# Second attention stage of a fused decoder kernel: probabilities turned by VectorE blocks and DMAs, head outputs two tiles behind the scores

## The reference, cut to what matters

```python
    x = x + _L0_xattn_ref(_layernorm(x, axis=-1), ctx_1024, mask_BxS2_bk0, L0_xattn_W_Q, L0_xattn_W_K, L0_xattn_W_V, L0_xattn_W_O)
...
        Q = _split_heads(X_Q @ W_Q, KEY_SIZE)
        K = _split_heads(X_KV @ W_K, KEY_SIZE)
        V = _split_heads(X_KV @ W_V, VALUE_SIZE)
        E = jnp.einsum('bhqd,bhkd->bhqk', Q, K)
        E = jnp.where(key_padding_mask[:, None, None, :], -jnp.inf, E)
        A = jax.nn.softmax(E / jnp.sqrt(jnp.float32(KEY_SIZE)), axis=-1)
        Yp = jnp.einsum('bhqk,bhkd->bhqd', A, V)
...
        Y = Yp.transpose(0, 2, 1, 3).reshape(b, sq, h * dv) @ W_O
```

## Time and profile before

| | us |
|---|---|
| runs | 3205.45, 3195.68, 3205.67 |
| median | 3205.45 |
| profiled execution, its time | 3192.96 |
| its span, first to last instruction | 3190.9 |
| TensorE busy in it | 3112.9 |
| VectorE, ScalarE, GpSimd busy | 2767.5, 2517.5, 2330.3 |
| mean granted TensorE clock, share of full | 0.993 |
| first queries matmul of the second stage | at 176.15 |
| first TensorE instruction of the third stage | at 553.67 |

### The profile page before, as it was taken

The page is one execution under the profiler, slowest core; times in us unless marked ns, Lnnn a source line. Parts: engine busy times, 40 slices in busy tenths (PEclk is TensorE's granted clock), DMA queues, the critical chain, the costliest instruction groups (busy, mean ns, idle before and its releaser), DMA issues.

```text
span 3190.9 us, 125347 instructions
## 1 busy us (share of the span) xinstructions
PE 3112.9 (98%) x51271; PEld 2450.5 (77%) x51271; DVE 2767.5 (87%) x5489; ACT 2517.5 (79%) x5156; POOL 2330.3 (73%) x3927
## 2 busy tenths in 40 slices
PE   7999999899999999999999999999999999999997
PEld 5677787577777777777777777777777777777776
DVE  6844444899999999999999999999999999999996
ACT  6856665588888888888888888888888888888886
POOL 6732222788888888888888888888888888888885
PEclk9999999999999999999999999999999999999998
DMA  4000000565555655555655566555565555555552
GB/s 111 3 7 8 8 8 5 119 129 108 108 109 121 123 121 110 111 109 122 125 108 108 109 124 126 115 111 110 114 126 122 109 107 109 109 108 117 114 117 60
DMA packets 280547, 310.51 MB, mean 97 GB/s; under 512 B 154281, under 2 KB 225582, under 8 KB 279982
## 3 DMA queue, kind: packets, MB, share of 16 engines
q0 software_dynamic: 58368, 201.36, 34.1%
q1 hardware_dynamic: 220892, 100.93, 12.7%
q10 hardware_dynamic: 722, 0.21, 0.0%
HBM read 23.63 MB, written 2.10 MB: 8 GB/s over the span
## 4 chain that ended last, share of the span: by engine, by line
PE 86%; DVE 4%; ACT 3%; issue 2%; POOL 2%; SPq 1%; DMA 1%; POOLq 0%; ACTq 0%; DVEq 0%
PE bank L1173 10%; PE bank L1195 10%; PE bank L1141 10%; PE bank L1255 10%; PE bank L1229 8%; PE bank L1112 8%; PE bank L1244 6%; PE bank L1214 5%; PE bank L1128 4%; PE bank L1152 3%; PE bank L728 2%; PE bank L741 2%; PE bank L750 2%; PE bank L805 2%; PE bank L1209 1%
## 5 line engine op out<-in xcount | busy, mean ns | idle before, releaser
L1435 DVE TENSOR_TENSOR RK<-bank,tables 128x1024 f32<-128x1024 f32 x384 | 468.5, 1224 | 83.0 <-ACT sq L1320 75.4
L1421 DVE TENSOR_TENSOR RQ<-bank,q_tables 128x1024 f32<-128x1024 f32 x384 | 451.3, 1217 | 25.8 <-ACT sq L1314 11.9
L1569 POOL TENSOR_TENSOR RK<-RK,rn 128x512 f32<-128x512 f32 x384 | 400.9, 1045 | 86.5 <-DMA RK<-RK 72.8
L1575 POOL TENSOR_TENSOR P<-P,rn 128x512 f32<-128x512 f32 x384 | 395.2, 1050 | 6.0 <-DVE P L1485 5.9
L1173 PE MATMUL bank<-WA,xcT 128*128 128x512 f32 x768 | 394.9, 596 | 2.5 <-DVE P L1485 2.4
L1287 ACT ACTIVATE V<-bank 128x512 f32<-128x512 f32 x384 | 230.5, 600 | 209.0 <-PE bank L1244 208.4
L1581 POOL TENSOR_TENSOR P<-P,inv_sum 128x512 f32<-128x512 f32 x384 | 393.5, 1045 | 0.0
L1195 PE MATMUL bank<-WV,xcT 128*128 128x512 f32 x768 | 391.6, 605 | 0.0
L1555 POOL DMA_DIRECT2D RQ<-RQ x384 | 387.4, 1313 | 2.3 <-issue 2.3
L1141 PE MATMUL bank<-xcT,WQ 128*128 128x128 f32 x3072 | 375.9, 276 | 4.8 <-ACT xcT L1287 4.8
L1561 POOL DMA_DIRECT2D RK<-RK x192 | 175.4, 913 | 280.7 <-DVE RK L1435 267.2
(11 more groups left out here) (169 smaller groups left out, 7341.0 us busy)
## 6 DMA issues: line engine op xcount, KB each, us to landing
RK<-RK POOLq DMA_DIRECT2D x192, 512.0 KB, 5.4
RQ<-RQ POOLq DMA_DIRECT2D x384, 256.0 KB, 6.6
Z<-Z SPq DMA_DIRECT2D x768, 64.0 KB, 4.1
WA<-in_wqkv SPq DMA_DIRECT2D x24, 256.0 KB, 2.9
ystat<-Y SPq DMA_DIRECT2D x192, 32.0 KB
ystat<-Y SPq DMA_DIRECT2D x384, 15.8 KB
ys<-Y SPq DMA_DIRECT2D x192, 32.0 KB
ys<-Y SPq DMA_DIRECT2D x384, 15.8 KB
```

The costliest lines, as they stand in the source:

```text
L1421: tt(both, src.unsqueeze(1).to_broadcast([128, 2, 8, SEQ]), m.q_tables[:, layer(t), :, :].unsqueeze(2).to_broadcast([128, 2, 8, SEQ]), ALU ...
L1435: tt(both, src.unsqueeze(1).to_broadcast([128, 2, 16, 32]), tab.unsqueeze(2).to_broadcast([128, 2, 16, 32]), ALU.mult).then_inc(s.rotated. ...
L1569: tt(part, part, wide(m.rn[:, t % 4, 16 + 8 * j:24 + 8 * j]), ALU.mult).then_inc(s.k_scaled.sem, 1)
L1575: tt(part, part, wide(m.rn[:, t % 4, a:16:2]), ALU.mult).then_inc(s.scaled.sem, 1)
```

## The change

Five things are changed in `cross_attention`, none elsewhere.

1. The eight transposes of P on TensorE and the two copies by ScalarE go. VectorE transposes P in blocks of 32x32, two instructions per tile, into BLOCKS, which lies in m.sq and has one buffer; SyncE moves the blocks into m.PT with eight DMAs per tile, two buffers. The transposes wait until the DMAs of the tile before have landed (p_moved).
2. `values` gives V with both sequences' 128 tokens on the partitions, two matmuls with 512 columns and a full 128-column left side.
3. `head_outputs` pairs rows by sequence, as the third stage does, runs two tiles behind the scores, and waits for p_moved.
4. `out_projection` runs three tiles behind, and `added`, `inverse_deviation` and `normalised` with it. Every loop is one round longer.
5. The turned inputs get the bank that the turned probabilities had, so they no longer wait for an OT copy. OT is written in the order in which the projection reads it.

The transposes are gone there, and one more round of head outputs and projection follows. The diff, cut to its core:

```diff
-    V_BANK, PT_BANK, PV_BANK = (b[5], b[1]), (b[6], b[7]), (b[2], b[4])
-    OUT, TURNED_IN = b[7], b[4]
+    V_BANK, PV_BANK = (b[5], b[1]), (b[2], b[4])
+    OUT, TURNED_IN = b[7], b[6]
+    BLOCKS = m.sq[:, 1, :].rearrange("p (a k n) -> p a k n", a=2, k=2)
+    PT = m.PT[:, :, :].rearrange("p t (a q n) -> p t a q n", a=2, q=2)
...
+        def probs_moved(t):
+            if exists(t):
+                sp.wait_ge(s.p_turned[1], t + 1)
+                sp.wait_ge(s.p_turned[0], t + 1)
+                at_least(sp, s.o, 2 * (t - 1))
+                for to in range(4):
+                    for q in range(2):
+                        frm = to - to % 2 + q
+                        sp.dma_start(PT[32 * to:32 * to + 32, t % 2, :, q, :], BLOCKS[32 * frm:32 * frm + 32, :, to % 2, :])\
+                            .then_inc(s.p_moved[t % 2], 16)
...
         for t in range(N):
             at_least(sp, s.x_turned, t - 3)
             sp.dma_start(m.ctx_sb[:, t % 4, :], ctx_tiles[t, :, :]).then_inc(s.ctx[t % 4], 16)
+            probs_moved(t - 2)
+        for t in range(N - 2, N):
+            probs_moved(t)
...
-                for j in range(2):
-                    pe.wait_ge(s.v_copied[j], t + 1)
-                    pe.wait_ge(s.p_copied[j], t + 1)
...
+                pe.wait_ge(s.v_copied[0], t + 1)
+                pe.wait_ge(s.v_copied[1], t + 1)
+                pe.wait_ge(s.p_moved[t % 2], 128 * (t // 2) + 128)
...
-        for i in range(N + 2):
+        for i in range(N + 3):
             inputs_turned(i)
-            out_projection(i - 2)
+            out_projection(i - 3)
...
-            probs_turned(i - 1, 1)
-            probs_turned(i - 1, 0)
             scores(i)
-            head_outputs(i - 1)
+            head_outputs(i - 2)
...
+        def probs_turned(t, a):
+            if exists(t):
+                dve.wait_ge(s.normal[a], t + 1)
+                at_least(dve, s.p_moved[(t - 1) % 2], 128 * ((t + 1) // 2))
+                blocks = m.P[:, t % 2, a * 512:(a + 1) * 512].rearrange("p (h k n) -> p k h n", k=2, n=32)
+                nc.vector.transpose(BLOCKS[:, a, :, :].rearrange("p k (h n) -> p k h n", n=32), blocks)\
+                    .then_inc(s.p_turned[a], 1)
```

More of the change, by code:

```diff
@@ L752, in keys @@
                 last.then_inc(s.k[j], 1)
-        def probs_turned(t, j):
-            if exists(t):
-                pe.wait_ge(s.normal[j], t + 1)
-                if j == 1:
-                    at_least(pe, s.y1, t)
-                for n in range(4):
-                    at = j * 512 + n * 128
-                    last = turned(PT_BANK[j][:, n * 128:(n + 1) * 128], m.P[:, t % 2, at:at + 128])
-                last.then_inc(s.p_turned[j], 1)
         def scores(t):
@@ L786, in head_outputs @@
             if exists(t):
-                for j in range(2):
-                    pe.wait_ge(s.v_copied[j], t + 1)
-                    pe.wait_ge(s.p_copied[j], t + 1)
-                for j in range(4):
-                    for bb in range(2):
-                        for e, a in ((0, 0), (1, 1), (0, 1), (1, 0)):
-                            rows, head = slice(64 * e, 64 * e + 64), slice(64 * a, 64 * a + 64)
-                            vals, probs = bb * 512 + j * 128 + a * 64, (4 * a + j) * 128 + bb * 64
-                            last = mm(PV_BANK[e][head, j * 128 + bb * 64:j * 128 + bb * 64 + 64],
-                                      m.V[rows, t % 2, vals:vals + 64], m.PT[rows, t % 2, probs:probs + 64],
-                                      start=True, stop=True)
-                            if j == 3 and bb == 1 and (e, a) in ((0, 1), (1, 0)):
-                                last.then_inc(s.o, 1)
@@ L801, in values @@
-        def values(t, bb):
-            if exists(t):
-                cols = WV.rearrange("p (j e n) -> p e j n", e=2, n=128)
-                for e in range(2):
-                    last = mm(V_BANK[bb][64 * e:64 * e + 64, :], m.ctxT[:, t % 2, bb * 64:bb * 64 + 64],
-                              cols[:, e, :, :], start=True, stop=True)
-                last.then_inc(s.v[bb], 1)
-        for i in range(N + 2):
+                pe.wait_ge(s.v_copied[0], t + 1)
+                pe.wait_ge(s.v_copied[1], t + 1)
@@ new lines, in head_outputs @@
+                pe.wait_ge(s.p_moved[t % 2], 128 * (t // 2) + 128)
+                for hp in range(PAIRS):
+                    for bb, a in ((0, 0), (1, 1), (0, 1), (1, 0)):
+                        rows, head, vals = slice(64 * bb, 64 * bb + 64), slice(64 * a, 64 * a + 64), (2 * hp + a) * 64
+                        last = mm(PV_BANK[bb][head, hp * 64:hp * 64 + 64], m.V[rows, t % 2, vals:vals + 64],
+                                  PT[rows, t % 2, a, :, hp * 32:hp * 32 + 32], start=True, stop=True)
+                        if hp == PAIRS - 1 and (bb, a) in ((0, 1), (1, 0)):
+                            last.then_inc(s.o, 1)
@@ L870, in _ @@
         m.cross_tail = lambda: normalised(N - 1)
-        for i in range(N + 3):
-            outputs_out(i - 2, 0)
+        for i in range(N + 4):
+            outputs_out(i - 3, 0)
             exponents(i - 1, 0)
@@ L969, in _ @@
         pool.memset(m.Z[:, :, :, :, :], 0.0)
-        for i in range(N + 2):
+        for i in range(N + 3):
             probs_scaled(i - 1, 1)
             probs_scaled(i - 1, 0)
-            inverse_deviation(i - 2)
+            inverse_deviation(i - 3)
 QUERIES, KEYS = 0, 1
```

33 lines of the change are left out of this document (17 added, 16 removed).

## The result

| | before | changed |
|---|---|---|
| median of 20 runs each, us | 3201.6 | 3208.7 |
| lowest and highest, us | 3195.0 to 3210.1 | 3200.5 to 3218.6 |
| profiled execution: span, us | 3190.9 | 3204.0 |

The ratio of the changed kernel to the kernel before is 1.0021, with a 95% interval of 1.0013 to 1.0029: **the change costs 7 us (4 to 9)**. Two later comparisons gave 1.0024 (1.0010 to 1.0038) and 1.0025 (1.0013 to 1.0037). The prediction said 3205 with no change beyond what a measurement can tell. The 7 us lie within the 0.3% that it called "same", but they are there, and they go the other way than its sum of -0.1 us.

The account below looks back on a forecast made before the run. It took the second stage to be held by TensorE's wait for the kT copy, then bound twice from mask to next queries. Terms -6.8 + 1.4 + 5.3 = -0.1 us, added to the 3205.45 median, gave about 3205; range 3190 to 3240.

Parts of the forecast that it names:

- the 0.3% that it called "same": Whole kernel: a measurement can tell about 0.3%, 9.6 us; a time within that, 3195 to 3218, had 0.74.
- its sum of -0.1 us: Whole kernel: mask gain -6.8, head +1.4 and tail +5.3 us together make -0.1 us.
- The gain at the mask, -6.8 us: Scores' mask matmul: without transposes it follows the kT copy by 0.14 us, gaining 0.22 us in each of 31 tiles.
- the lower bound of this term: Mask: nothing gained, if the gap behind the transposes is the issue of the six waits ahead of the scores.
- the upper end of its own case: Whole kernel: the change doesn't do what it says, for instance since waits make the mask's gap; own upper end +12.5 us.
- The bound: Second stage, before the mask: the transposes fill time in which TensorE would wait for ScalarE's kT copy.
- The first rival: Second stage: TensorE's work is the bound after all, the whole 1.16 us per tile comes back, 3176 us; chance 0.06.
- The double bound behind the scores: Mask to next queries, 6.42 us: bound twice, by TensorE's work and by the chain scores, VectorE, ScalarE.
- The head, +1.4 us: Second stage's start: tile 2, now without projection, repeats tile 1's idle time and low clock, -0.3 + 1.7 us.
- The tail, +5.3 us: Second stage's end: last head outputs come 8.3 us after the statistics, with 6.9 us of DMAs, where 3.0 were.
- What was to cost nothing: Second stage: values by token, strided OT copies and moved context loads at 0; GpSimd held up by transposes had chance 0.05.
- the middle, 3205: Whole kernel: the forecast time, the sum added to the median of 3205.45 us, giving 3205.4, about 3205.

## Why the prediction was wrong

*The gain at the mask, -6.8 us: wrong, measured 0.* The step that failed is "I take 0.22, since its row shows the very wait". The row was tile 0's, and it differs from all others in more than the transposes: it lacks the two waits for the subtractions, and with them the two wait instructions behind the blocking one, 0.11 us each, that all other tiles have in both kernels. The prediction had the right cause as the lower bound of this term ("if the gap behind the transposes is the issue of the six waits ahead of the scores") and named it again as the upper end of its own case; it chose the wrong end. With the waits reordered, before and changed kernel alike gain, 0.18 and 0.22 us per tile, 7 to 9 us in all.

*The bound: right.* The transposes filled a wait. The first rival, TensorE's work as the bound (3176), was rightly kept at 0.06 for this order. The double bound behind the scores was right as well: filling the hole on TensorE alone changed nothing.

*The head, +1.4 us: too large.* From first to fourth queries it was 217.75 - 181.68 = 36.07 us against 212.13 - 176.15 = 35.98, so 0.1 us. The queries and keys of tile 2 didn't run in the low clock a second time.

*The tail, +5.3 us: right in the first profile (5.05), 6.2 us in two later ones.* In the first of those the mean granted clock from 540 to 560 us is 0.79 (0.84 in the first profile, 0.83 before), and the last head outputs too ran in the part at 1.2 GHz in place of 2.4: 1.99 us in place of 1.16. The moves as its cause were right only in part: left out, they give back 1.9 to 4.5 us of 6.9, since the projection of the tile before is close behind them. That the larger distance between scores and head outputs is the rest is argued from the order and not shown by itself; the old way for the last tile, which takes away both, brings the end stretch to 21.15 us, from 26.20.

*What was to cost nothing*, values by token, OT copies with a stride, context loads behind the moves and GpSimd beside the transposes, left no trace in the steady tile. In the first profile eight issues took 5.1 to 6.5 us, 5.8 in the median, that is 0.63 to 0.82 each, where 0.68 was taken; they landed after 2.0 us in the median as taken, 3.6 at most.

*The sum* with the measured terms is 0 + 0.1 + 5.05 to 6.2, so 5 to 6 us. That this lies in the measured 4 to 9 is luck in part: by the profiles the second stage is only 2.5 us longer, since 2.6 to 4.0 us came back in tiles of unusual length, for which the prediction has no term, and 4 to 5 us are outside the stage that it looked at. The range of 3190 to 3240 held the time, and the bound of 0.3% holds it too. That the middle, 3205, was only 4 us off the measured 3208.7 is luck as well: it was built on a median of three runs, 3205.45, where twenty gave 3201.6. The change itself was off by 7 us, -0.1 against +7, and the term of the mask is 6.8.

## What to carry to other kernels

Before a row is used as the price of a wait, compare the instruction's whole list of waits there and at the place in question; put the wait that blocks last, and look in the trace how many wait instructions are left behind it. Work taken from the busiest engine is worth its time only where that engine never waits: first find whether the hole that it leaves can be filled, and since several in-order queues hold it open, they must be reordered together (here three edits on two engines turned a loss of 7 us into a gain of 30 to 37). A path with a longer latency is paid in full where a pipeline drains; the last tile can keep the old, short path.

## What the runs showed of the hardware

- Each wait instruction behind the blocking one cost TensorE some 0.1 us: two of them put the matmul 0.36 us behind the end of the releasing copy, in place of 0.14 us with none. One such instruction carried up to two waits; fulfilled waits ahead of the blocking one, or on the same instructions as others, cost nothing that the tile shows (10.94 us with four more ahead and without).
- SyncE's price for a move within SBUF goes by the move and not by its bytes: 0.63 to 0.70 us for 32 KB, 0.63 to 0.82 us for 64 KB.
- Two programs that differ in four fulfilled waits per tile differed by 5 us of 3200 side by side, and by some 8 us by their ratios to the kernel before on different chips, more than their profiles explain. A difference of 0.2% between two kernels is not yet one of the change that one has in mind.
